# A DLRM tower on one core: whole-array products for three of four batch tiles, other shares of one-hot work, more queues and another order of the layers

## The reference

```
e = stack([tbl_f[ids[:, f]] for f in range(27)], axis=1)      # 512 x 27 x 128
z = einsum('bnd,bmd->bnm', e, e)[:, i, j]                     # i < j: 351 pairs
h = concatenate([z, dense_ctx], axis=1)                       # 512 x 367
h = maximum(h @ W_top1 + b_top1, 0)                           # 512
h = maximum(h @ W_top2 + b_top2, 0)                           # 256
y = h @ W_top3                                                # 1
```

## Time and profile before

| | before |
|---|---|
| median of 3 runs | 138.52 us |
| profiled execution, its own time | 138.44 us |
| its span, first to last instruction | 136.5 us |
| mean granted clock of TensorE, share of full | 0.912 |
| busy: PE, DVE, ACT, POOL | 116.4, 77.6, 65.2, 76.3 us |

### The profile page before, as it was taken

The page is one execution under the profiler, slowest core; times in us unless marked ns, Lnnn a source line. Parts: engine busy times, 40 slices in busy tenths (PEclk is TensorE's granted clock), DMA queues, the critical chain, the costliest instruction groups (busy, mean ns, idle before and its releaser), DMA issues.

```text
span 136.5 us, 2480 instructions
## 1 busy us (share of the span) xinstructions
PE 116.4 (85%) x1016; PEld 93.8 (69%) x1016; DVE 77.6 (57%) x67; ACT 65.2 (48%) x106; POOL 76.3 (56%) x92
## 2 busy tenths in 40 slices
PE   5679989999698987989895697757899989999894
PEld 5546767777486775867674465535699969899791
DVE  2499999999999999999602020200435011531221
ACT  4099998999949696596030203002422111151021
POOL 2187888788788787888889989987000000001300
PEclk9999999999999999999999755555579999999999
DMA  3987787888675869941121112551144410003300
GB/s 58 325 340 175 245 255 243 275 199 264 225 237 168 243 143 362 352 94 38 38 56 44 38 38 58 179 102 53 45 126 111 106 27 0 0 5 130 74 0 1
DMA packets 15103, 18.67 MB, mean 137 GB/s; under 512 B 8767, under 2 KB 10905, under 8 KB 14964
## 3 DMA queue, kind: packets, MB, share of 16 engines
q1 hardware_dynamic: 12932, 14.20, 34.5%
q0 software_dynamic: 2016, 4.06, 10.6%
q10 hardware_dynamic: 144, 0.26, 1.1%
HBM read 16.74 MB, written 1.77 MB: 136 GB/s over the span
## 4 chain that ended last, share of the span: by engine, by line
PE 39%; DVE 36%; issue 16%; DMA 6%; ACT 1%; SPq 0%; ACTq 0%; DVEq 0%
DVE hot L432 24%; PE psG L332 18%; DVE parts L437 11%; PE psH L347 5%; PE psH L377 4%; DMA pick_ids<-in_picked_ids 3%; PE psT L295 3%; PE psG L315 3%; PE psG L359 3%; DMA pair_blocks<-gram 2%; PE psH L390 2%; DMA zT<-pair_blocks 1%; ACT gram L526 1%; DVE ET L422 1%; SPq L162 0%
## 5 line engine op out<-in xcount | busy, mean ns | idle before, releaser
L273 POOL DMA_INDIRECT rows<-in_tbl,ids_sb x60 | 65.4, 1090 | 19.7 <-issue 15.1
L315 PE MATMUL psG<-hot,parts 128*128 128x512 f32 x216 | 55.4, 403 | 7.4 <-DVE hot L432 2.9
L315 PEld LDWEIGHTS psG<-hot,parts 128*128 128x128 f32 x216 | 38.6, 188 | 20.8 <-DVE hot L432 6.5
L432 DVE TENSOR_TENSOR hot<-pick_ids,psH 128x1536 fp32r<-128x1536 int32 (+1 forms) x24 | 47.4, 2014 | 3.3 <-DMA pick_ids<-in_picked_ids 3.3
L332 PE MATMUL psG<-ET 128*52 128x54 f32 x512 | 25.1, 248 | 8.1 <-issue 7.0
L332 PEld LDWEIGHTS psG<-ET 128*52 128x52 f32 x512 | 20.6, 154 | 13.2 <-issue 11.8
L445 DVE COPY gram<-psG 128x432 f32<-128x432 f32 x8 | 7.2, 903 | 30.4 <-remote 19.8
L526 ACT COPY gram<-psG 128x432 f32<-128x432 f32 x8 | 7.2, 898 | 28.4 <-remote 19.8
L170 POOL DMA_DIRECT2D zT<-pair_blocks x2 | 1.7, 869 | 30.5 <-DMA pair_blocks<-gram 30.5
L437 DVE TENSOR_TENSOR parts<-table,parts 128x1024 fp32r<-128x1024 f32 (+1 forms) x12 | 16.2, 1352 | 0.0
L514 ACT ACTIVATE hot<-pick_ids,row_no 128x512 fp32r<-128x512 int32 x24 | 16.2, 727 | 0.0
(11 more groups left out here) (27 smaller groups left out, 40.5 us busy)
## 6 DMA issues: line engine op xcount, KB each, us to landing
table<-in_tbl SPq DMA_DIRECT2D x6, 640.0 KB
table<-in_tbl SPq DMA_DIRECT2D x6, 512.0 KB, 6.5
pick_ids<-in_picked_ids SPq DMA_DIRECT2D x11, 256.0 KB, 3.9
pair_blocks<-gram SPq DMA_DIRECT2D x8, 216.0 KB, 2.4
w_sb<-in_w SPq DMA_DIRECT2D x1, 1024.0 KB
rows<-in_tbl,ids_sb POOLq DMA_INDIRECT x60
w_sb<-in_w SPq DMA_DIRECT2D x1, 512.0 KB
zT<-pair_blocks SPq DMA_DIRECT2D x7, 63.0 KB
```

The source lines that it names most:

```text
L273: pool.indirect_dma_start(out=rows[:, n % RING, x, :], out_offset=None, in_=gathered_tables[f], in_offset=bass.IndirectOffsetOnAxis(ap=ids ...
L315: last = pe.matmul(psP[:, k % 2, :], parts[:, k % 2, x, c, :], hot[:, k % 2, c, :], start=x == 0 and c == 0, stop=x == 1 and c == CH[k] - 1)
L432: dve.tensor_tensor(hot[:, k % 2, first:end, :], pick_ids[:, k % TABLES, :].unsqueeze(1).to_broadcast(shape), numbers.unsqueeze(2).to_broa ...
```

## The change

For tiles 0 to 2 (`WIDE = 3`) a product takes four samples at once: 108 rows by 108 columns in the whole array, of which the four diagonal blocks of 27 x 27 are used. A bank holds four of them (432 columns as before), a tile has 32 products in four units. `gram` gets one more dimension, the copies take the same 432 columns of a bank, and the scratch writes of such a tile are four DMAs of 32 partitions. Samples are numbered otherwise inside a tile on the host, so that `ET` stays contiguous. Tile 3 keeps the column tiles.

ACT makes 3 of the one-hot chunks where a table has 10 (2 of 8 as before), and has one Relu for all its chunks. POOL writes the scratch tile after each of the first ten quads too. Of the scratch writes half go to ACT's queue, at ("write", t) in the list; ACT also reads two chunks of tile 0, and chunk 1 of tile 3 in place of POOL. Layer 1 of tile 0 is done chunk by chunk, and its three layers use the banks of `psG`; tile 1's layer 1 then comes ahead of tile 0's layer 3.

```diff
+    WIDE = 3
+    GB = [4 if t < WIDE else 8 for t in range(T)]
+    U = [GH // (2 * GB[t]) for t in range(T)]
+    FIRST = [sum(U[:t]) for t in range(T + 1)]
+    WRITES = [Q if t < WIDE else S for t in range(T)]
...
-    BY_ACT = [2] * FP
+    BY_ACT = [2 if chunks == min(CH) else 3 for chunks in CH]
...
+    BY_CHUNK = (0, T - 1)
+    SP_READS = [(0, 1), (0, 1, 2, 3), (0, 1, 2, 3), (0, 2)]
+    ACT_READS = [(2, 3), (), (), (1,)]
...
-        steps = units(0) + quads(9, 10) + units(1) + quads(10, 12) + units(2) + quads(12, 13)
-        steps += mlp(0) + quads(13, 14) + [("layer3", 0)] + mlp(1) + quads(14, 16) + [("layer3", 1)] + units(3)
-        steps += mlp(2) + [("chunk", 0), ("layer3", T - 2), ("chunk", 1), ("chunk", 2),
+        steps = units(0) + [("write", 0)] + quads(9, 10) + units(1) + [("write", 1)] + quads(10, 12) + [("read", 0)]
+        steps += units(2) + [("write", 2)] + quads(12, 13) + mlp(0) + quads(13, 14)
+        steps += [("layer1", 1), ("layer3", 0), ("layer2", 1), ("layer2_end", 1)] + quads(14, 16) + [("layer3", 1)]
+        steps += units(3) + [("write", 3)]
+        steps += mlp(2) + [("read", T - 1), ("chunk", 0), ("layer3", T - 2), ("chunk", 1), ("chunk", 2),
...
-                for x in range(S):
+                for x in range(WRITES[t] // 2):
                     write_blocks(sp, t, x)
-                sp.wait_ge(blocks_out[t], 16 * S)
-                for c in range(NC) if t < T - 1 else (0, 2):
+                sp.wait_ge(blocks_out[t], 16 * WRITES[t])
+                for c in SP_READS[t]:
                     read_pairs(sp, t, c)
...
-                    if n >= FIRST_PAUSED:
+                    if n >= FIRST_PAUSED or x == len(QUADS[q]) - 1:
...
             def product_unit(m):
...
-                    for x in range(GB):
-                        for h in range(H):
-                            group = ET[:, t, GH * h + GU * u + GB * bank + x, :, :].rearrange("d f s -> d (f s)")
-                            last = pe.matmul(psG[R * h:R * h + S * J, m % 2, bank, S * F * x:S * F * (x + 1)],
-                                             group[:, 0:S * J], group, start=True, stop=True)
+                    for x in range(GB[t]):
+                        g = H * (GB[t] * (2 * u + bank) + x)
+                        for h in array_tiles(t):
+                            if t < WIDE:
+                                group = ET[:, t, g:g + H, :, :].rearrange("d h f s -> d (h f s)")
+                                rows_in, cols = H * S * F, H * S * F
+                            else:
+                                group = ET[:, t, g + h, :, :].rearrange("d f s -> d (f s)")
+                                rows_in, cols = S * J, S * F
+                            last = pe.matmul(psG[R * h:R * h + rows_in, m % 2, bank, cols * x:cols * (x + 1)],
+                                             group[:, 0:rows_in], group, start=True, stop=True)
...
             def layer1(t):
-                else:
+                if t > 1:
                     pe.wait_ge(y_ready, t)
...
-            def last_layer1(c):
+            def layer1_chunk(t, c):
                 if c == 0:
-                    pe.wait_ge(gram_dve, U * T)
-                    pe.wait_ge(gram_act, U * T)
+                    products = FIRST[T if t == T - 1 else T - 1]
+                    pe.wait_ge(gram_dve, products)
+                    pe.wait_ge(gram_act, products)
...
             def layer3(t):
+                elif t < T - 1:
+                    pe.wait_ge(y_ready, t)
...
             def make_last_hot(k):
...
-                for x, c in enumerate(chunks):
-                    act.wait_ge(distance_ready, sum(BY_ACT[:k]) + x + 1)
-                    act.activation(hot[:, k % 2, c, :], hot[:, k % 2, c, :], ACT.Relu, bias=1.0, scale=-1.0
-                                   ).then_inc(last_hot_ready, 1)
+                act.wait_ge(distance_ready, sum(BY_ACT[:k + 1]))
+                last = hot[:, k % 2, chunks[0]:CH[k], :]
+                act.activation(last, last, ACT.Relu, bias=1.0, scale=-1.0).then_inc(last_hot_ready, 1)
...
+            def write_half(t):
+                act.wait_ge(gram_dve, FIRST[t + 1])
+                act.wait_ge(gram_act, FIRST[t + 1])
+                for x in range(WRITES[t] // 2, WRITES[t]):
+                    write_blocks(act, t, x)
+            def read_half(t):
+                act.wait_ge(blocks_out[t], 16 * WRITES[t])
+                for c in ACT_READS[t]:
+                    read_pairs(act, t, c)
```

More of the change, by code:

```diff
@@ L84, in dlrm_tower @@
         ET = sb("ET", [P, T, G, F, S])
-        gram = sb("gram", [P, 2, S, F, GH])
+        gram = sb("gram", [P, 2, H, S, F, GH])
         zT = sb("zT", [P, T, NC, P])
@@ L191, in quad_views, with unit_place, multiplied_by, array_tiles @@
             return (ET[:, n // NQ, :, fs[0]:fs[-1] + 1, :],
-                    psT[:, n % 2, 0:len(fs), :].rearrange("d f (s g) -> d g f s", s=S))
-        def unit_views(m, bank):
[L196 to L199, removed]
+                    psT[:, n % 2, 0:len(fs), :].rearrange("d f (g s) -> d g f s", s=S))
+        def unit_place(m):
+            t = max(x for x in range(T) if FIRST[x] <= m)
+            return t, m - FIRST[t]
+        def multiplied_by(m, bank, h):
+            return 2 * (m - (0 if h == 0 else FIRST[WIDE])) + bank + 1
+        def array_tiles(t):
+            return range(1 if t < WIDE else H)
+        def unit_views(m, bank):
+            t, u = unit_place(m)
+            g = GB[t] * (2 * u + bank)
+            if t < WIDE:
+                return (gram[:, t % 2, :, :, :, g:g + GB[t]].rearrange("p h s j g -> p g h j s"),
+                        psG[:, m % 2, bank, 0:GB[t] * H * S * F].rearrange("p (g h j s) -> p g h j s", h=H, j=F, s=S))
+            return (gram[:, t % 2, 0, :, :, g:g + GB[t]].rearrange("p s j g -> p g j s"),
+                    psG[:, m % 2, bank, 0:GB[t] * S * F].rearrange("p (g j s) -> p g j s", j=F, s=S))
         def units(t):
-            return [("unit", U * t + u) for u in range(U)]
+            return [("unit", m) for m in range(FIRST[t], FIRST[t + 1])]
         def quads(a, b):
@@ L225, in _ @@
                     sp.wait_ge(hot_ready, 2 * (k - TABLES + 1))
-                    sp.wait_ge(last_hot_ready, sum(BY_ACT[:k - TABLES + 1]))
+                    sp.wait_ge(last_hot_ready, k - TABLES + 1)
                 if k >= 1:
@@ L313, in pick @@
                             else:
-                                pe.wait_ge(last_hot_ready, sum(BY_ACT[:k]) + c - own + 1)
+                                pe.wait_ge(last_hot_ready, k + 1)
                         last = pe.matmul(psP[:, k % 2, :], parts[:, k % 2, x, c, :], hot[:, k % 2, c, :],
@@ L346, in layer1 @@
                     for c in range(NC):
-                        last = pe.matmul(psH[:, n // 2, n % 2, :], w1_sb[0:ROWS[c], c, P * n:P * (n + 1)],
+                        last = pe.matmul(h1_psum(t, n), w1_sb[0:ROWS[c], c, P * n:P * (n + 1)],
                                          zT[0:ROWS[c], t, c, :], start=c == 0, stop=c == NC - 1)
@@ L405, in _ @@
                     transposes(x)
+                elif step == "layer1" and x in BY_CHUNK:
+                    for c in range(NC):
+                        layer1_chunk(x, c)
                 elif step == "layer1":
@@ L414, in _ @@
                 elif step == "chunk":
-                    last_layer1(x)
+                    layer1_chunk(T - 1, x)
         @block.vector
@@ L440, in unit_copies @@
             def unit_copies(m):
[L441 to L444, removed]
+                t, u = unit_place(m)
+                if t >= 2:
+                    dve.wait_ge(blocks_out[t - 2], 16 * WRITES[t - 2])
+                for h in array_tiles(t):
+                    dve.wait_ge(multiplied[h], multiplied_by(m, 0, h))
                 dve.tensor_copy(*unit_views(m, 0)).then_inc(gram_dve, 1)
@@ L557, in _ @@
                     quad_copy(x)
+                elif step == "write":
+                    write_half(x)
+                elif step == "read":
+                    read_half(x)
                 elif step in ("layer1", "relu1"):
@@ L611 @@
         "in_dense": np.ascontiguousarray(np.asarray(inputs["dense_ctx"]).T),
-        "in_ids": np.ascontiguousarray(ids[:, gather].reshape(-1, 128, len(gather)).transpose(1, 0, 2)),
-        "in_picked_ids": np.ascontiguousarray(ids[:, pick].T),
+        "in_ids": np.ascontiguousarray(inner[:, gather].reshape(-1, 128, len(gather)).transpose(1, 0, 2)),
+        "in_picked_ids": np.ascontiguousarray(inner[:, pick].T),
         "in_w1": w1_chunks,
```

64 lines of the change are left out of this document (36 added, 28 removed).

## The result

The changed kernel takes 140.36 us (median of 20 runs, 138.66 to 141.78) against 138.53 in as many runs of the kernel before (136.99 to 154.54): 1.0125 times, interval 1.009 to 1.016, so slower by about 1%. 124 was forecast, 120.5 to 130. Executions more than 1.5% above the fastest of their kernel count in all medians and ranges, but not in the ratios and their intervals. The profiled execution took 140.18, its span is 138.4.

The account below looks back on a forecast made before the run. DVE was taken to bound the picks, then a PE starved of instructions, then the tail. Picks -3.2, stretch -10.6 and tail -0.5 summed to -14.3 us: span 122.2, time 124.1, range 120.5 to 130.

Parts of the forecast that it names:

- the dips allowed: In the stretch of products and layers, 1.0 us allowed for local dips in PE's supply.
- Balanced work: In the picks, DVE's ten-chunk pick falls from 5.79 to 5.26 us: -3.2 us over six picks.
- Pauses: In the first ten quads, pauses move the last gather from 93.7 to about 96.3 us, at no cost.
- Whole-array products: In tiles 0 to 2, 64 pairs instead of 128, 94 ns each: 6.0 us a tile (6.0 to 7.1).
- the array is nearly always fed: Between the picks' and gathers' ends, supply gives 280 pairs against 259 wanted, so PE stays busy at 2.4 GHz.
- a stock plus a limited supply: PE beside gathers: 42 pairs in stock when products begin, then 6 to 9 pairs per us until gathers end.
- the prediction's doubt about instruction fetch: On PE, the sparse windows were held to disagree with the skill's rule that instruction fetch is mostly hidden.
- Copies: After the products, 0.90 us copies on DVE and ACT, against 0.75 us per bank and 1.5 per unit, stay hidden.
- Writes on ACT: Two scratch writes after tile 1's copies, ahead of quad 11's copy, cost 1.0 us on the path.
- Rival C: The clock still falls, from dips or the wait for ACT's writes before tile 2: 3 to 5 us, 128; chance 0.09.
- Rival D: Beside gathers PE is held for a share of time, 0.66 busy, not by instruction count: 143.3 us; chance 0.04.
- The forecast of the sign: For the whole kernel: 0.91 faster, 0.03 within 1%, 0.06 slower.

Follow-up runs that it names:

- part 2: The changed kernel with POOL's 22 late gathers replaced by plain loads of consecutive table rows by SP's queue: 126.95 us, 0.908.
- part 7: The kernel before with its 22 gathers of quads 10 to 15 replaced by plain loads by SP's queue: 121.44 us, 0.858.
- without both parts: The changed kernel with old one-hot shares and no early pauses: 139.06 us, 0.986.
- best version: The changed kernel with one pause after each gather up to quad 9 and two after each later one: 134.09 us, 0.957.
- three pauses: The changed kernel with old shares and three scratch writes instead of one after each of the last 22 gathers: 137.48 us, 0.995.

## Why the prediction was wrong

Against the sum of the prediction (span 122.2) the profiled span has 16.2 us more. Tile 3's products start at 119.34 instead of 104.0, and the 15.3 us lie as follows: products start at 69.25 instead of 67.3, +2.0; tile 0 takes 9.9 instead of 6.0, at a granted clock of 0.83, +3.9; tile 1 10.6, +4.6; the wait behind quad 11 is 4.85 instead of 1.8, +3.0; tile 2 takes 8.85, at a granted clock of 0.69 behind that wait, +2.9; the dips allowed, -1.0. From there on the layers took 14.7 us where 14.7 was written. The tail is 0.9 us longer than forecast.

- *Balanced work*: DVE's pick right (5.27), the picks' end right (PE 67.0); ACT did not set the pace. Of the 3.2 us, 2.0 were lost at the hand-over to the products, and worse: the denser picks are what PE can't bear beside dense gathers (the shares alone 151.28, no early pauses 161.72, against the pauses alone 140.18).
- *Pauses*: costed at 0, and 0 by themselves. That they were what kept the new shares alive I had not seen.
- *Whole-array products*: the price was right, 96 to 98 ns a pair and 6.3 us a tile where nothing holds PE (no late gathers, part 2), inside the 6.0 to 7.1 written. **The step that failed** is "the array is nearly always fed". I read the starvation as a supply of instructions, "a stock plus a limited supply" of 8.5 pairs per us, and held 280 pairs against the 259 wanted. Tiles 0 and 1 got 64 pairs each in 9.9 and 10.6 us, 6.0 to 6.5 per us. What limits the changed kernel is how soon PE's finished work is known to others while POOL gathers. Why PE stops in the middle of a bank in the kernel before, as one might expect of a supply, stays open; it is gone with the gathers, with the same instructions (part 7), so the prediction's doubt about instruction fetch falls too.
- *Copies*, "buffered twice, so hidden": a round trip of 0.76 + 0.25 + 3.1 + 0.9 us over four banks of 8 pairs gives 1.3 us a bank and more as the lag grows, 1.44 measured (76.71 to 78.15), not 0.75. The row was there: DVE's copies stood idle 19.8 us for "remote". The copy of 76.50 in the trace of before, 3.5 us late, was there as well. I took that for PE's slowness.
- *Writes on ACT*: 1.50 us for two, not 1.0. Without late gathers the same wait is 2.5 us, so late signals make 2.3 of the 4.85.
- *Rival C* (the clock falls behind the wait for ACT's writes) came as well: 4.84 us without work, then 0.50, and the 2.9 us of tile 2. It had 3 to 5 us and a chance of 0.09.
- *Rival D* (PE held for a share of time) came nearest: its 0.66 of the rate gives 9.1 us a tile, 9.9 and 10.6 came. I gave it 0.04, since the first pairs ran dense. In the changed kernel they may, until PE needs a bank back; in the kernel before PE stopped after 56 pairs with banks left, and why there is not shown. The clock, its other half, fell for less long: the mean is 0.86 from 67 to 104 us. The forecast of the sign hung on this.

## What to carry to other kernels

Before counting what a stretch would take with fewer or larger instructions, measure the gap from a producer's end to its consumer's start there: if it is microseconds with the consumer idle, the stretch is paid in round trips, and the more often work is handed over through small buffers, the longer it gets. Look too whether the producer's stops fall on buffer boundaries; those that don't have another reason. A gain taken from the engine that set the pace can push another over a limit that the old pace had just kept; try such a part alone.

## What the runs showed of the hardware

While POOL issued indirect DMAs mostly 1.25 us apart, 20 matmuls of 512 columns in 5.8 us left PE's signals on time in the trace of the kernel before, but not in that without both parts, where a pick done at 47.45 is copied at 50.06. In 5.3 us they led to pieces of 14.7 us (no early pauses) and 17.2 us (shares alone) in which PE did nothing. At 1.5 us apart the lag grew from nothing to 3 to 4 us under dense products. At 1.9 us (68.43 to 70.33, best version) and at 2.3 us (68.87 to 71.20, three pauses) the signals of tiles 0 and 1 came within 0.1 us, as they did without gathers. DVE's and ACT's signals weren't late: PE started 0.05 us behind their copies. The Trainium skill, SBUF — State Buffer, "Who interferes with whom", says that only the port pair of VectorE and GpSimd causes contention and that TensorE and ScalarE wait on nobody. For the ports nothing here contradicts it. As a rule on whole engines it differs from what was measured, and the measurement decides: TensorE stood still for 14.7 us at a time beside GpSimd's gathers, and tiles of 9.9 us took 6.3 without them.

By what path a gather holds up PE and its signals no run here shows; nor was it tried whether the writing of the descriptors or the transfers do it. Nothing here says either why some executions pile up among the picks and others don't.
